# Decay and cosine products written back into PSUM; sine product and low parts of weights on GpSimd; new orders

## The chip, the core and the metric

The kernel runs on one core of one Trainium2 chip. The metric is the time of one execution on the device in microseconds (us), lower is better. The kernel before took 289.08 us, the median of three runs (288.9, 289.08, 290.38).

## What is computed

A pre-norm transformer block in float32 on x of shape (4, 256, 256), four sequences of 256 tokens, with linear ("lightning") attention. There are 16 query heads, 4 key and value heads of 128, rotary positions and a decay for each head.

```python
h = layernorm(x)
q, k, v = h @ wq.T, h @ wk.T, h @ wv.T           # 16, 4 and 4 heads of 128
q, k = rope(q), rope(k)                          # z * cos + rot(z) * sin; rot swaps the halves of 128
# chunked scan in the reference; the same as, for each head with lam = 2**(-8*i/16):
o[i] = sum over j <= i of exp(-lam * (i - j)) * (q[i] . k[j]) * v[j]
x = x + concat(o) @ wo.T
h = layernorm(x)
hidden = fwht(silu(h @ W1.T) * (h @ W3.T))       # Walsh-Hadamard transform over 1024
x = x + hidden @ W2.T
```

## The kernel before

Matrix products keep float32 accuracy by splitting each operand into a high part (a copy rounded to the matmul format fp32r) and a low part (the operand minus its high part). Each product is then three matmuls: high by high, high by low, low by high (`product`, L264 to L266). So every tensor that goes into TensorE (PE) costs a copy on ScalarE (ACT) for the high part and a subtraction on VectorE (DVE) or GpSimd (POOL) for the low part.

The tokens are worked in two halves of 512 (two sequences each). A **unit** u = 0..15 is one pair of heads of one half: u = 8c + p. There are eight PSUM banks. Projections (the items X, K, Q, V in the list `LIN`) land in banks 0 and 1 by turns after the start, in all eight at the start; the scores of a unit stand in banks 2 to 4, the attention output in bank 5, the output projection in 6 and 7. The pipeline of a unit is:

- PE projects the two query heads of unit u + 2 (`queries(u)`), and in even units the key head too (`key(u)`, heads are shared by two units). The item for p = 5 also turns the next normalized half (`turned`). An item may be projected only when the item two places earlier has left its bank (`lin_free`).
- Rotary: ACT copies the two halves of the bank crosswise into `rope_b` (`swap`, L494 and L495). DVE multiplies the bank by the cosine into `rope_a` (L752) and `rope_b` by the sine in place (L753) (`rotate`). POOL adds the two into `qk` (`rope_add`, L629). ACT takes the high part (L500), POOL the low part (`low_rope`, L636).
- Scores: PE writes three banks. DVE multiplies each by the decay table into `p_raw` (`mask`, L775). ACT takes the high part `p_hi` (L507). The low part `p_lo` comes from DVE for the first two (L780), from POOL for the third, S_FIRST1 (L641).
- PE multiplies by the values (`attend`), ACT and DVE split the output (`o_hi` L511, `o_lo` L785), and PE projects it (`project_out`).
- Weights come in 16 chunks of 128x1024. ACT takes the high part (L474) and DVE the low part (L727), one chunk at the end of each of units 0 to 5 and of 9, 11, 12 and 13. PE may use a chunk when `w_lo_done` has reached it: the queries projected in unit 2 need chunk 5, those of unit 4 need chunk 7.

The order on each engine is written out by hand: each engine's block walks over the same loop of units, with helpers called in a fixed order, and every engine executes strictly in that order. An instruction whose semaphore is not there holds all behind it on its engine. After the units comes the feed-forward part, in which PE is fed without rotary work.

## Time and profile before

| | |
|---|---|
| timed runs | 288.9, 289.08, 290.38 us; median 289.08 |
| span of the profiled execution | 287.6 us |
| PE busy | 261.9 us, 91% (1480 matmuls) |
| DVE busy | 229.2 us, 80% |
| POOL busy | 175.0 us, 61% |
| ACT busy | 164.5 us, 57% |
| granted TensorE clock | full in all 40 slices |

The page gives no time for the profiled execution other than its span, which lies 1.5 us under the median of the timed runs. The share of busy time is a mean over very different stages: up to about 11 us everything waits for the first loads and the norm, from there to about 210 us run the 16 units, in which four engines work together, and after that PE is busy nearly without a break while the others idle. DVE shows 9 in every tenth digit from 7% to 40% of the span, PE mostly 7 to 9 there. A busy digit says nothing on who waits for whom; for that the waits and the starts of single instructions are read.

### The profile page before, as it was taken

How to read it: one execution, taken by the hardware profiler on the slowest of the kernel's cores; microseconds unless marked ns; L12 is line 12 of the kernel's file. 1: busy time of each engine (PE TensorE's matmuls, PEld its weight loads, DVE VectorE, ACT ScalarE, POOL GpSimd, SP SyncE). 2: the span in 40 equal slices, each digit the busy share in tenths (PEclk: the TensorE clock that was granted, in tenths of full speed). 3: DMA queues.
4: the chain of work that ended last, by engine and by line, in shares of the span. 5: the costliest groups of instructions: out<-in, count | busy, mean ns of one | idle time of the engine just before them, and what ended most of it. 6: DMA issues, size and time to landing. Idle time of an engine off the chain costs nothing.

```text
span 287.6 us, 4155 instructions
## 1 busy us (share of the span) xinstructions
PE 261.9 (91%) x1480; PEld 226.0 (79%) x1480; DVE 229.2 (80%) x324; ACT 164.5 (57%) x271; POOL 175.0 (61%) x117
## 2 busy tenths in 40 slices
PE   0897898997997999889999979969999999999995
PEld 0685677885896888778898878859888889988885
DVE  2878999999999999876989999999667686234323
ACT  2586776669475686556668658486445453033320
POOL 1049799789975978955687897969795610000000
PEclk9999999999999999999999999999999999999999
DMA  7694020211102020000001002200000000110002
GB/s 269 228 370 135 2 74 1 73 32 43 73 2 74 5 70 1 0 2 0 1 13 63 0 2 73 74 0 2 0 2 0 0 3 0 39 36 0 2 0 73
DMA packets 5203, 13.23 MB, mean 46 GB/s; under 512 B 576, under 2 KB 2112, under 8 KB 5184
## 3 DMA queue, kind: packets, MB, share of 16 engines
q1 hardware_dynamic: 4752, 12.65, 12.4%
q10 hardware_dynamic: 432, 0.33, 0.3%
q8 instruction: 12, 0.20, 0.3%
q14 instruction: 7, 0.06, 0.1%
HBM read 11.93 MB, written 1.05 MB: 45 GB/s over the span
## 4 chain that ended last, share of the span: by engine, by line
PE 34%; DVE 34%; POOL 13%; issue 12%; ACT 4%; DMA 1%; DVEq 0%; SPq 0%; POOLq 0%; ACTq 0%
PE bank L264 11%; PE bank L265 11%; PE bank L266 11%; DVE p_lo L780 7%; DVE rope_b L753 6%; POOL qk L629 6%; DVE p_raw L775 5%; DVE rope_a L752 5%; POOL q_hid L636 4%; DVE xn L721 3%; DVE w_lo L727 3%; DVE o_lo L785 2%; POOL k_lo L636 2%; ACT p_hi L507 1%; DMA x_sb<-in_x 1%
## 5 line engine op out<-in xcount | busy, mean ns | idle before, releaser
L629 POOL TENSOR_TENSOR qk<-rope_a,rope_b 128x512 f32<-128x512 f32 x40 | 66.9, 1687 | 18.9 <-DVE rope_b L753 18.8
L264 PE MATMUL bank<-xt_hi,w_hi 128*128 128x512 f32 x144 | 58.5, 407 | 5.2 <-DVE rope_a L752 3.8
L265 PE MATMUL bank<-xt_lo,w_hi 128*128 128x512 f32 x144 | 57.2, 397 | 0.0
L266 PE MATMUL bank<-xt_hi,w_lo 128*128 128x512 f32 x144 | 57.1, 397 | 0.0
L636 POOL TENSOR_TENSOR q_hid<-qk,q_hid 128x512 fp32r<-128x512 f32 x32 | 48.6, 1529 | 4.0 <-ACT q_hid L500 3.9
L780 DVE TENSOR_TENSOR p_lo<-p_raw,p_hi 128x512 fp32r<-128x512 f32 x32 | 40.1, 1255 | 3.0 <-ACT p_hi L507 2.6
L507 ACT ACTIVATE p_hi<-p_raw 128x512 fp32r<-128x512 f32 x48 | 30.1, 626 | 15.4 <-DVE p_raw L775 14.8
L264 PEld LDWEIGHTS bank<-xt_hi,w_hi 128*128 128x128 f32 x144 | 27.6, 192 | 13.5 <-DVE rope_a L752 5.5
L641 POOL TENSOR_TENSOR p_lo<-p_raw,p_hi 128x512 fp32r<-128x512 f32 x16 | 25.9, 1617 | 20.2 <-ACT p_hi L507 20.1
L753 DVE TENSOR_TENSOR rope_b<-rope_b,sin_sb 128x512 f32<-128x512 f32 x40 | 36.8, 919 | 0.0
L265 PE MATMUL bank<-w_lo,o_hi 128*128 128x256 f32 x128 | 36.2, 283 | 0.0
L266 PE MATMUL bank<-w_hi,o_lo 128*128 128x256 f32 x128 | 36.2, 283 | 0.0
L264 PE MATMUL bank<-w_hi,o_hi 128*128 128x256 f32 x128 | 36.1, 282 | 0.0
L494 ACT ACTIVATE rope_b<-bank 64x512 f32<-64x512 f32 x40 | 23.8, 596 | 17.6 <-POOL qk L629 12.5
L500 ACT ACTIVATE q_hid<-qk 128x512 fp32r<-128x512 f32 x32 | 20.1, 628 | 23.0 <-POOL qk L629 22.3
L266 PEld LDWEIGHTS bank<-xt_hi,w_lo 128*128 128x128 f32 x144 | 27.6, 192 | 6.1
L752 DVE TENSOR_TENSOR rope_a<-bank,cos_sb 128x512 f32<-128x512 f32 x40 | 27.1, 678 | 6.0 <-ACT rope_b L495 5.9
L775 DVE TENSOR_TENSOR p_raw<-bank,decay_sb 128x512 f32<-128x512 f32 x48 | 31.4, 677 | 0.5 <-PE bank L266 0.4
L265 PEld LDWEIGHTS bank<-xt_lo,w_hi 128*128 128x128 f32 x144 | 27.7, 192 | 5.0
L264 PE MATMUL bank<-q_hid,k_hi 128*128 128x512 f32 (+1 forms) x64 | 22.5, 352 | 5.2 <-POOL k_lo L636 5.1
L799 DVE TENSOR_TENSOR rope_b<-bank,rope_a 128x512 f32<-128x512 f32 x16 | 11.0, 689 | 19.6 <-ACT rope_a L518 19.6
L518 ACT ACTIVATE rope_a<-bank 128x512 f32<-128x512 f32 x16 | 9.6, 600 | 27.6 <-PE bank L266 27.6
(70 smaller groups left out, 611.6 us busy)
## 6 DMA issues: line engine op xcount, KB each, us to landing
w_raw<-in_w SPq DMA_DIRECT2D x6, 512.0 KB, 3.2
w_raw<-in_wq SPq DMA_DIRECT2D x4, 512.0 KB, 4.8
decay_sb<-in_decay SPq DMA_DIRECT2D x4, 512.0 KB, 5.9
w_raw<-in_wo SPq DMA_DIRECT2D x4, 512.0 KB, 3.3
x_sb<-in_x SPq DMA_DIRECT2D x4, 256.0 KB, 4.6
out<-x_sb SPq DMA_DIRECT2D x8, 128.0 KB, 1.8
w_raw<-in_wk SPq DMA_DIRECT2D x1, 512.0 KB, 4.8
w_raw<-in_wv SPq DMA_DIRECT2D x1, 512.0 KB, 6.6
```

The source lines that it names most:

```text
L264: pe.matmul(o, a_hi, b_hi, start=first, stop=False, skip_group_check=shared)
L265: pe.matmul(o, a_hi, b_lo, start=False, stop=False, skip_group_check=shared)
L266: return pe.matmul(o, a_lo, b_hi, start=False, stop=last, skip_group_check=shared)
L494: act.activation(rope_b[0:h, r % 2, :], lin_bank(n)[h:P], ACT.Copy)
L507: act.activation(p_hi[:, s, :], p_raw[:, n % 2, :], ACT.Copy).then_inc(p_hi_done, 1)
L629: pool.tensor_tensor(qk[:, r % 2, :], rope_a[:, r % 2, :], rope_b[:, r % 2, :], ALU.add).then_inc(rope_sum, 1)
L636: pool.tensor_tensor(lo, qk[:, r % 2, :], hi.bitcast(F32), ALU.subtract).then_inc(rope_lo, 1)
L641: pool.tensor_tensor(p_lo[:, s, :], p_raw[:, n % 2, :], p_hi[:, s, :].bitcast(F32), ALU.subtract).then_inc(p_lo_pool, 1)
L752: dve.tensor_tensor(a, src, c, ALU.mult).then_inc(lin_free, 1)
L753: dve.tensor_tensor(b, b, s, ALU.mult).then_inc(rope_parts, 1)
L775: dve.tensor_tensor(dst, src, table, ALU.mult).then_inc(mask_done, 1)
L780: dve.tensor_tensor(p_lo[:, s, :], p_raw[:, n % 2, :], p_hi[:, s, :].bitcast(F32), ALU.subtract).then_inc(p_lo_dve, 1)
```

## The change

Four things change.

1. The decay product of the first two score banks and the cosine product are written back into the PSUM bank that they come from. `p_hi`, `p_lo` (first two) and the rotary add then read PSUM. `rope_a` is gone (the feed-forward part's buffer is now called `gate`), and a score bank is free only after its low part (`p_lo_dve`), a projection bank only after the rotary add.
2. The rotary add moves from POOL to DVE (`rotated`), the sine product from DVE to POOL (`times_sine`).
3. The low parts of the weight chunks from chunk 3 on move from DVE to POOL (`low_weights` on POOL), at the end of POOL's unit.
4. All four engines get new orders.

```diff
-        rope_a = sb("rope_a", [P, 2, TOK])
+        gate = sb("gate", [P, 2, TOK])
         rope_b = sb("rope_b", [P, 2, TOK])
...
@@ -311,8 +291,10 @@
                 ks, qs = p // PPG % 2, p % 2
                 needed = max(ROPE_NO[("Q", c, 2 * p + 1)], ROPE_NO[("K", c, p // PPG)])
                 pe.wait_ge(rope_lo, needed + 1)
-                if u:
-                    pe.wait_ge(mask_done, 3 * (u - 1) + s + 1)
+                if u and s == S_FIRST1:
+                    pe.wait_ge(mask_done, 3 * u)
+                elif u:
+                    pe.wait_ge(p_lo_dve, 2 * (u - 1) + s + 1)
...
-                if b == 0:
-                    pe.wait_ge(p_lo_dve, 2 * (u + 1))
-                else:
+                pe.wait_ge(p_lo_dve, 2 * (u + 1))
+                if b:
                     pe.wait_ge(p_lo_pool, u + 1)
...
@@ -489,14 +470,14 @@
                 n, r = LIN_NO[item], ROPE_NO[item]
                 act.wait_ge(lin_full, n + 1)
                 if r >= 2:
-                    act.wait_ge(rope_sum, r - 1)
+                    act.wait_ge(lin_free, LIN_NO[ROPE[r - 2]] + 1)
...
             def high_rope(item):
                 r = ROPE_NO[item]
-                act.wait_ge(rope_sum, r + 1)
+                act.wait_ge(lin_free, LIN_NO[item] + 1)
                 act.activation(rope_dst(item)[0], qk[:, r % 2, :], ACT.Copy).then_inc(rope_hi, 1)
 
             def high_p(u, s):
@@ -504,7 +485,8 @@
                 act.wait_ge(mask_done, n + 1)
                 if u and s == S_SECOND:
                     act.wait_ge(o_full, 2 * u)
-                act.activation(p_hi[:, s, :], p_raw[:, n % 2, :], ACT.Copy).then_inc(p_hi_done, 1)
+                src = p_raw[:, u % 2, :] if s == S_FIRST1 else s_bank[s][:]
+                act.activation(p_hi[:, s, :], src, ACT.Copy).then_inc(p_hi_done, 1)
...
-            high_weights(3)
             swap(("K", 0, 0))
             swap(("Q", 0, 0))
+            high_rope(("K", 0, 0))
             high_v(0, 0)
-            high_rope(("K", 0, 0))
             swap(("Q", 0, 1))
+            high_rope(("Q", 0, 0))
             high_v(0, 1)
-            high_rope(("Q", 0, 0))
+            high_weights(3)
             swap(("Q", 0, 2))
+            high_rope(("Q", 0, 1))
             high_v(0, 2)
-            high_rope(("Q", 0, 1))
             swap(("Q", 0, 3))
+            high_rope(("Q", 0, 2))
             high_v(0, 3)
-            high_rope(("Q", 0, 2))
-            high_p(0, S_FIRST0)
             high_rope(("Q", 0, 3))
-            high_p(0, S_SECOND)
             for u in range(UNITS):
-                if u:
-                    before = queries(u - 1)
-                    fill(key(u - 1) + turned(u - 1))
-                    for item in before[:1]:
-                        high_rope(item)
-                    high_p(u, S_FIRST0)
-                    for item in before[1:]:
-                        high_rope(item)
-                    high_o(u - 1, 1)
-                    high_p(u, S_SECOND)
-                fill(values(u)[:2] + queries(u)[:1])
+                fill(key(u - 1) + turned(u - 1) if u else [])
+                high_p(u, S_FIRST0)
+                high_p(u, S_SECOND)
                 for item in key(u - 1) if u else []:
                     high_rope(item)
-                fill(queries(u)[1:])
+                if u:
+                    high_o(u - 1, 1)
+                fill(values(u)[:1])
                 high_p(u, S_FIRST1)
+                fill(values(u)[1:2] + queries(u))
                 if u in (UNITS - 2, UNITS - 1):
                     silu(u - UNITS + 2)
                 fill(values(u)[2:3])
+                for item in queries(u)[:1]:
+                    high_rope(item)
                 high_o(u, 0)
+                for item in queries(u)[1:]:
+                    high_rope(item)
                 fill(values(u)[3:])
                 if unit_chunk(u) is not None:
                     high_weights(unit_chunk(u))
...
-            def rope_add(item):
+            def times_sine(item):
                 r = ROPE_NO[item]
-                pool.wait_ge(rope_parts, r + 1)
-                if r >= 2:
-                    pool.wait_ge(rope_lo, r - 1)
-                pool.tensor_tensor(qk[:, r % 2, :], rope_a[:, r % 2, :], rope_b[:, r % 2, :],
-                                   ALU.add).then_inc(rope_sum, 1)
+                pool.wait_ge(swapped, r + 1)
+                b = rope_b[:, r % 2, :].rearrange("p (b t) -> p b t", b=BH)
+                pool.tensor_tensor(b, b, sin_sb[:].unsqueeze(1).broadcast_to([P, BH, SEQ]),
+                                   ALU.mult).then_inc(sin_done, 1)
...
-            def low_p(u, s):
-                n = 3 * u + s
-                pool.wait_ge(p_hi_done, n + 1)
-                pool.tensor_tensor(p_lo[:, s, :], p_raw[:, n % 2, :], p_hi[:, s, :].bitcast(F32),
+            def low_weights(n):
+                _, _, at = CHUNKS[n]
+                pool.wait_ge(w_lo_done, n)
+                pool.wait_ge(w_hi_done, n + 1)
+                pool.tensor_tensor(w_lo[:, at:at + CH], w_raw[:, n % SLOTS, :], w_hi[:, at:at + CH].bitcast(F32),
+                                   ALU.subtract).then_inc(w_lo_done, 1)
+
+            def low_p(u):
+                pool.wait_ge(p_hi_done, 3 * (u + 1))
+                pool.tensor_tensor(p_lo[:, S_FIRST1, :], p_raw[:, u % 2, :], p_hi[:, S_FIRST1, :].bitcast(F32),
                                    ALU.subtract).then_inc(p_lo_pool, 1)
...
-            rope_add(("K", 0, 0))
-            rope_add(("Q", 0, 0))
+            pool.wait_ge(tables_loaded, 48)
+            times_sine(("K", 0, 0))
+            times_sine(("Q", 0, 0))
             low_rope(("K", 0, 0))
-            rope_add(("Q", 0, 1))
+            times_sine(("Q", 0, 1))
             low_rope(("Q", 0, 0))
+            times_sine(("Q", 0, 2))
             low_rope(("Q", 0, 1))
-            rope_add(("Q", 0, 2))
-            rope_add(("Q", 0, 3))
+            times_sine(("Q", 0, 3))
             low_rope(("Q", 0, 2))
+            low_weights(3)
             low_rope(("Q", 0, 3))
             for u in range(UNITS):
-                if u:
-                    before = queries(u - 1)
-                    for item in before[:1]:
-                        low_rope(item)
-                    if u % PAIRS == 3:
-                        inverse_deviation(u // PAIRS + 1)
-                    for item in key(u - 1):
-                        rope_add(item)
-                    for item in before[1:] + key(u - 1):
-                        low_rope(item)
-                low_p(u, S_FIRST1)
+                before = key(u - 1) if u else []
+                for item in before:
+                    times_sine(item)
+                if u % PAIRS == 3:
+                    inverse_deviation(u // PAIRS + 1)
+                for item in before:
+                    low_rope(item)
+                low_p(u)
                 for item in queries(u):
-                    rope_add(item)
+                    times_sine(item)
+                for item in queries(u):
+                    low_rope(item)
+                if unit_chunk(u) is not None:
+                    low_weights(unit_chunk(u))
...
-            def rotate(item):
+            def times_cosine(item):
 
                 n, r = LIN_NO[item], ROPE_NO[item]
                 dve.wait_ge(swapped, r + 1)
+                o = lin_bank(n)[:].rearrange("p (b t) -> p b t", b=BH)
+                dve.tensor_tensor(o, o, cos_sb[:].unsqueeze(1).broadcast_to([P, BH, SEQ]),
+                                  ALU.mult).then_inc(cos_done, 1)
+
+            def rotated(item):
+
+                n, r = LIN_NO[item], ROPE_NO[item]
+                dve.wait_ge(cos_done, r + 1)
+                dve.wait_ge(sin_done, r + 1)
                 if r >= 2:
-                    dve.wait_ge(rope_sum, r - 1)
-                src, a, b = (m.rearrange("p (b t) -> p b t", b=BH)
-                             for m in (lin_bank(n)[:], rope_a[:, r % 2, :], rope_b[:, r % 2, :]))
-                c, s = (tb[:].unsqueeze(1).broadcast_to([P, BH, SEQ]) for tb in (cos_sb, sin_sb))
-                dve.tensor_tensor(a, src, c, ALU.mult).then_inc(lin_free, 1)
-                dve.tensor_tensor(b, b, s, ALU.mult).then_inc(rope_parts, 1)
+                    dve.wait_ge(rope_lo, r - 1)
+                dve.tensor_tensor(qk[:, r % 2, :], lin_bank(n)[:], rope_b[:, r % 2, :],
+                                  ALU.add).then_inc(lin_free, 1)
...
-                if s == S_FIRST1:
-                    dve.wait_ge(p_lo_dve, 2 * u + 1)
-                elif u and s == S_FIRST0:
-                    dve.wait_ge(p_lo_dve, 2 * u)
-                elif u:
-                    dve.wait_ge(p_lo_pool, u)
+                if s == S_FIRST1 and u >= 2:
+                    dve.wait_ge(p_lo_pool, u - 1)
...
-                    dst = p_raw[:, n % 2, :].rearrange("p (b h t) -> p b h t", b=BH, h=2)
                 else:
                     src = s_bank[s][:].rearrange("p (h t) -> p h t", h=2)
-                    dst = p_raw[:, n % 2, :].rearrange("p (h t) -> p h t", h=2)
+                dst = p_raw[:, u % 2, :].rearrange("p (h t) -> p h t", h=2) if s == S_FIRST1 else src
                 dve.tensor_tensor(dst, src, table, ALU.mult).then_inc(mask_done, 1)
...
             def low_p(u, s):
                 n = 3 * u + s
                 dve.wait_ge(p_hi_done, n + 1)
-                dve.tensor_tensor(p_lo[:, s, :], p_raw[:, n % 2, :], p_hi[:, s, :].bitcast(F32),
+                dve.tensor_tensor(p_lo[:, s, :], s_bank[s][:], p_hi[:, s, :].bitcast(F32),
                                   ALU.subtract).then_inc(p_lo_dve, 1)
...
+            times_cosine(("K", 0, 0))
+            times_cosine(("Q", 0, 0))
             fill(START[2:5])
-            low_weights(3)
-            fill(START[5:])
-            mask(0, S_FIRST0)
-            mask(0, S_SECOND)
-            low_p(0, S_FIRST0)
-            low_p(0, S_SECOND)
+            for h in range(1, 4):
+                times_cosine(("Q", 0, h))
+                fill([("Q", 0, h), ("V", 0, h)])
             for u in range(UNITS):
+                before = key(u - 1) if u else []
+                mask(u, S_FIRST0)
+                mask(u, S_SECOND)
+                for item in before:
+                    times_cosine(item)
+                low_p(u, S_FIRST0)
+                fill(before + turned(u - 1) if u else [])
+                low_p(u, S_SECOND)
                 if u:
-                    mask(u, S_FIRST0)
-                    mask(u, S_SECOND)
-                    fill(key(u - 1) + turned(u - 1))
-                    low_p(u, S_FIRST0)
                     low_o(u - 1, 1)
-                    low_p(u, S_SECOND)
                 fill(values(u)[:1])
                 mask(u, S_FIRST1)
                 if u == PAIRS + 1:
                     add_attention(0, 1)
-                fill(values(u)[1:2] + queries(u))
+                fill(values(u)[1:2])
+                for item in queries(u):
+                    times_cosine(item)
+                fill(queries(u))
...
-                if unit_chunk(u) is not None:
-                    low_weights(unit_chunk(u))
```

POOL around unit 0 and 1, before. `qk<-rope_a,rope_b` is the rotary add, `q_hid` and `k_lo` take low parts.

```order
L641 TENSOR_TENSOR p_lo<-p_raw,p_hi 128x512
L629 TENSOR_TENSOR qk<-rope_a,rope_b 128x512 x2
L636 TENSOR_TENSOR q_hid<-qk,q_hid 128x512
L629 TENSOR_TENSOR qk<-rope_a,rope_b 128x512
L636 TENSOR_TENSOR q_hid<-qk,q_hid 128x512
L636 TENSOR_TENSOR k_lo<-qk,k_hi 128x512
L641 TENSOR_TENSOR p_lo<-p_raw,p_hi 128x512
```

POOL at the same place in the changed kernel. `rope_b<-rope_b,sin_sb` is the sine product.

```order
L620 TENSOR_TENSOR w_lo<-w_raw,w_hi 128x1024
L614 TENSOR_TENSOR q_hid<-qk,q_hid 128x512
L625 TENSOR_TENSOR p_lo<-p_raw,p_hi 128x512
L607 TENSOR_TENSOR rope_b<-rope_b,sin_sb 128x512 x2
L614 TENSOR_TENSOR q_hid<-qk,q_hid 128x512 x2
L620 TENSOR_TENSOR w_lo<-w_raw,w_hi 128x1024
L607 TENSOR_TENSOR rope_b<-rope_b,sin_sb 128x512
L614 TENSOR_TENSOR k_lo<-qk,k_hi 128x512
L625 TENSOR_TENSOR p_lo<-p_raw,p_hi 128x512
```

Between two low parts `p_lo` there now stands a chunk of weights, ahead of the key's sine product; both query low parts stand ahead of the chunk.

DVE in unit 1 (from the two decay products on), before.

```order
L775 TENSOR_TENSOR p_raw<-bank,decay_sb 128x512 x2
L752 TENSOR_TENSOR rope_a<-bank,cos_sb 128x512
L753 TENSOR_TENSOR rope_b<-rope_b,sin_sb 128x512
L780 TENSOR_TENSOR p_lo<-p_raw,p_hi 128x512
L785 TENSOR_TENSOR o_lo<-bank,o_hi 128x512
L780 TENSOR_TENSOR p_lo<-p_raw,p_hi 128x512
L775 TENSOR_TENSOR p_raw<-bank,decay_sb 128x512
L752 TENSOR_TENSOR rope_a<-bank,cos_sb 128x512
L753 TENSOR_TENSOR rope_b<-rope_b,sin_sb 128x512
```

DVE in unit 1 of the changed kernel, from the key's cosine product on.

```order
L735 TENSOR_TENSOR bank<-bank,cos_sb 128x512
L769 TENSOR_TENSOR p_lo<-bank,p_hi 128x512
L745 TENSOR_TENSOR qk<-bank,rope_b 128x512
L769 TENSOR_TENSOR p_lo<-bank,p_hi 128x512
L774 TENSOR_TENSOR o_lo<-bank,o_hi 128x512
L764 TENSOR_TENSOR p_raw<-bank,decay_sb 128x512
L735 TENSOR_TENSOR bank<-bank,cos_sb 128x512 x2
L745 TENSOR_TENSOR qk<-bank,rope_b 128x512 x2
L774 TENSOR_TENSOR o_lo<-bank,o_hi 128x512
```

The key's add (`qk<-bank,rope_b`), which needs POOL's sine product, now stands ahead of the second `p_lo`, of `o_lo` and of the third decay product. The same holds for the queries' two adds and the `o_lo` behind them.

ACT at the start of the changed kernel, from the swap of the second query on: the high part of weight chunk 3 now stands behind the second values' high part; before it stood ahead of all swaps.

```order
L475 ACTIVATE rope_b<-bank 64x512
L476 ACTIVATE rope_b<-bank 64x512
L481 ACTIVATE q_hid<-qk 128x512
L465 ACTIVATE v_hid<-bank 128x512
L455 ACTIVATE w_hi<-w_raw 128x1024
L475 ACTIVATE rope_b<-bank 64x512
L476 ACTIVATE rope_b<-bank 64x512
```

Every following swap at the start stands behind that chunk.

## Rows read from the trace of the kernel before

**Rows 1.** Busy time by engine in three stretches; columns as the first line says.

```profile
core 0: us, PE busy (x) PEld busy (x) DVE busy (x) ACT busy (x) POOL busy (x), PEclk, DMA share, GB/s
10.76:96.66 85.90, 77.50 (x399) 64.11 (x399) 82.03 (x106) 61.23 (x100) 67.75 (x43) 1.00 0.24 87
96.66:194.70 98.04, 92.66 (x538) 80.53 (x537) 90.30 (x122) 65.16 (x111) 77.79 (x50) 1.00 0.07 22
194.70:287.60 92.90, 89.57 (x540) 79.80 (x538) 51.74 (x83) 34.55 (x58) 28.11 (x20) 1.00 0.04 12
```

**Rows 2.** What PE waited for, 10.76 to 96.66: us, times, longest.

```profile
PE bank L264 <- POOL k_lo L636: 2.7, 2, 1.6
PE bank L264 <- DVE rope_a L752: 2.1, 3, 1.7
```

**Rows 3.** Groups of the page: shapes, count, busy us, mean ns, idle before, releaser.

```profile
L629 POOL TENSOR_TENSOR qk<-rope_a,rope_b 128x512 f32<-128x512 f32 x40 | 66.9, 1687 | 18.9 <-DVE rope_b L753 18.8
L636 POOL TENSOR_TENSOR q_hid<-qk,q_hid 128x512 fp32r<-128x512 f32 x32 | 48.6, 1529 | 4.0 <-ACT q_hid L500 3.9
L780 DVE TENSOR_TENSOR p_lo<-p_raw,p_hi 128x512 fp32r<-128x512 f32 x32 | 40.1, 1255 | 3.0 <-ACT p_hi L507 2.6
L641 POOL TENSOR_TENSOR p_lo<-p_raw,p_hi 128x512 fp32r<-128x512 f32 x16 | 25.9, 1617 | 20.2 <-ACT p_hi L507 20.1
L753 DVE TENSOR_TENSOR rope_b<-rope_b,sin_sb 128x512 f32<-128x512 f32 x40 | 36.8, 919 | 0.0
L494 ACT ACTIVATE rope_b<-bank 64x512 f32<-64x512 f32 x40 | 23.8, 596 | 17.6 <-POOL qk L629 12.5
L500 ACT ACTIVATE q_hid<-qk 128x512 fp32r<-128x512 f32 x32 | 20.1, 628 | 23.0 <-POOL qk L629 22.3
```

**Rows 4.** The same by line and shape: weights, and the low part that reads PSUM.

```profile
L727 DVE TENSOR_TENSOR w_lo<-w_raw,w_hi 128x1024 fp32r<-128x1024 f32 x14 | 22.2, 1588 | 0.5 <-ACT w_hi L474 0.5
L785 DVE TENSOR_TENSOR o_lo<-bank,o_hi 128x512 fp32r<-128x512 f32 x32 | 21.8, 680 | 2.3 <-ACT o_hi L511 2.1
L474 ACT ACTIVATE w_hi<-w_raw 128x1024 fp32r<-128x1024 f32 x14 | 14.6, 1051 | 4.1 <-DMA w_raw<-in_wk 3.1 <-DMA w_raw<-in_wq 1.0
```

**Rows 5.** POOL, single instructions: start, us, instruction, idle before and releaser.

```profile
42.93 1.68 POOL L629 TENSOR_TENSOR qk<-rope_a,rope_b 128x512 f32<-128x512 f32 x1 [0.63 <-DVE rope_b L753]
...
65.11 1.02 POOL L622 TENSOR_TENSOR rstd<-var_eps,minus_half 128x4 f32<-128x4 f32 x1
...
204.70 1.29 POOL L641 TENSOR_TENSOR p_lo<-p_raw,p_hi 128x512 fp32r<-128x512 f32 x1 [1.90 <-ACT p_hi L507]
205.95 1.30 POOL L659 TENSOR_TENSOR xn<-w_raw 128x512 f32<-128x512 f32 x1
```

**Rows 6.** POOL's low part of the third scores: of units 0, 2 and 5.

```profile
35.49 1.62 POOL L641 TENSOR_TENSOR p_lo<-p_raw,p_hi 128x512 fp32r<-128x512 f32 x1 [1.90 <-ACT p_hi L507]
...
58.66 1.30 POOL L641 TENSOR_TENSOR p_lo<-p_raw,p_hi 128x512 fp32r<-128x512 f32 x1 [2.51 <-ACT p_hi L507]
...
96.57 1.75 POOL L641 TENSOR_TENSOR p_lo<-p_raw,p_hi 128x512 fp32r<-128x512 f32 x1
```

**Rows 7.** ACT at the start: its swap of the first query.

```profile
16.25 0.60 ACT L494 ACTIVATE rope_b<-bank 64x512 f32<-64x512 f32 x1 [0.34 <-PE bank L266]
```

**Rows 8.** PE, single matmuls: start, us, instruction, idle before and releaser.

```profile
25.96 0.50 PE L264 MATMUL bank<-w_hi,xt_hi 128*128 128x512 f32 x1 [1.46 <-DVE v_hid L739]
...
52.36 0.39 PE L264 MATMUL bank<-xt_hi,w_hi 128*128 128x512 f32 x1
...
57.95 0.50 PE L264 MATMUL bank<-xt_hi,w_hi 128*128 128x512 f32 x1
...
94.92 0.34 PE L277 MATMUL bank<-ident_sb,xn 128*128 128x128 f32 x1
...
96.66 0.50 PE L264 MATMUL bank<-q_hid,k_hi 128*128 128x512 f32 x1
```

**Rows 9.** DVE's low part of weight chunk 5.

```profile
50.32 1.71 DVE L727 TENSOR_TENSOR w_lo<-w_raw,w_hi 128x1024 fp32r<-128x1024 f32 x1
```

25 lines of the change are left out of this document (12 added, 13 removed).

## The prediction, made before the changed kernel ran

> **What bounds the kernel now.** I read the busy time by stretch first. It cuts the run in three after a start of 10.8 us: the first six units (10.76 to 96.66), units 6 to 13 (to 194.70) and the rest [rows 1]. PE is idle for 85.90 - 77.50 = 8.4 us in the first, 98.04 - 92.66 = 5.4 in the second and 92.90 - 89.57 = 3.3 in the last. So PE is already the main bound, and all that a relief of the other engines can win is about 8.4 + 5.4 = 13.8 us, plus some tenths behind. Next, the waits of PE: in the first stretch it waits for POOL's low part of the key and for DVE's cosine product, by which a projection bank comes free, 4.8 us together [rows 2]. DVE, at 82.03 of 85.90 us, has no slack there, POOL some (67.75). The groups show why DVE is full: its operations with both inputs in SBUF are stretched (1255 ns for p_lo, 919 for the sine product), while the same size read from PSUM takes 680 [rows 3, 4]. POOL is stretched as well: an add takes 1.68 us beside DVE's work and such an operation follows the one before by 1.25 (205.95 - 204.70) when alone [rows 5].
>
> **Part by part: busy time.** DVE loses 40 sine products of 919 ns (36.8 us) and 11 of 14 weight chunks of 1588 ns (17.5 us). It gains 40 adds of about 0.65 (26 us), since they read a bank, and its 32 p_lo fall from 1255 to about 650 ns (19 us). Sum: about 47 us less [rows 3, 4]. A sine product takes the add's place on POOL one for one (40 each). POOL gets 11 chunks. No row shows a 128x1024 on POOL: the lower bound is 1.25 us (one 128x512), the upper 3.4 (two at 1.69); I take two uncontended ones, 2.5, since nothing in DVE's new steady work reads two SBUF inputs. So POOL: 96 operations at 1.25 in place of 141 us (66.9 + 48.6 + 25.9, the 8 key low parts besides), plus 27.5. Its total hardly changes; only its content does. PE's and ACT's work is the same. Busy time alone would therefore say faster. The page "SBUF — State Buffer" of the Trainium skill (section "Who interferes with whom") says that a DVE instruction with two SBUF inputs contends with a GpSimd one that reads SBUF and one with at most one SBUF input does not. The trace agrees (1.68 against 1.25). Were it otherwise, the POOL steps below would grow by 0.35 each. The skill's "GPSIMD Engine Reference" gives 4497 ns for 2048 elements of a float32 add (section "Reconciling with measured numbers"), an estimate of 2.25 us for a chunk; no trace here shows it, and the sum would be 1 us smaller by it.
>
> **Part by part: the chain.** What counts is which engine holds which in its order. Steps: POOL 1.25, DVE on a bank 0.65, ACT copy 0.63, ACT swap 2 x 0.6 = 1.2, ACT high part of a chunk 1.05 [rows 3 to 5], and 0.05 from a step on one engine to the next on another. I follow POOL's low part p_lo of the third scores from unit to unit; before, it starts at 35.49, 58.66 and 96.57 in units 0, 2 and 5: 61.1 us from 0 to 5 [rows 6].
>
> Interval without a key ahead (into units 2 and 4), from the moment its high part is there: two swaps 2.4 (now behind that high part), the second cosine product 0.65 (ahead of the first add), add 0.65 = 3.7; high parts of query and output 1.25, o_lo 0.65 = 5.6; two decay products 1.3; ACT's second p_hi 0.63, p_lo 0.65, o_lo 0.65, third decay product 0.65, its high part 0.63 = 10.1; with ten hand-overs 10.5 us.
>
> Interval with a key (into units 1, 3 and 5), on POOL: p_lo, two sine products 3.75; a bubble of 0.6, since the first query's high part comes only 3.7 + 0.63 in; two low parts 2.5; the weight chunk 2.5; the key's sine product 1.25 = 10.6. Only then DVE adds the key (0.65), and behind that add stand p_lo, o_lo and the third decay product: key's high part 0.63, o_hi 0.63, o_lo 0.65, product 0.65, high part 0.63 = 14.4, with few hand-overs 14.6 us. This is the step that I hold decisive: the chunk sits ahead of the key's sine product, and the add that waits for it sits ahead of the next unit's scores on DVE.
>
> Sum from unit 0 to 5: 3 x 14.6 + 2 x 10.5 + the rstd of unit 3, 1.0 [rows 5], and some statistics 0.5 = 66.3, against 61.1: 5.2 us later. POOL waits in it, so its spare time does not help.
>
> The start: swap of the first query at 16.25 [rows 7], done 17.45; cosine product and the key's add 1.3, key's high part and first values 1.23, swap 1.2, high parts of query and values 1.2, chunk 3 on ACT 1.05 (it stood ahead of all swaps), swap 1.2, sine product 1.25, add and low part of the third values 1.3 = 27.2 to 27.5 with hand-overs. PE's last values wait for that; they ran at 25.96 [rows 8]: 1.4 late. From there values 1.4, their high and low part 1.3, two decay products 1.3, p_hi 0.63, p_lo 0.65, product 0.65, high part 0.63: the first POOL p_lo at about 34.4, 1.1 us before its 35.49, since DVE's contended p_lo pair is gone. So unit 5's p_lo starts at 34.4 + 66.3 = 100.7.
>
> PE at the end of unit 5: the first turn of the normalized half needs the bank of unit 5's first query, free only after its add, 3.9 behind: 104.6. Before, this turn ran at 94.92 and the scores of unit 6 followed at 96.66 [rows 8]: 1.74 later, so now 106.3, 9.7 us late. Steps queued on one engine run a little closer than I set them (0.60 for 0.65), so I take 8.5. Bounds: -8.4 (all of PE's idle time gone) and 8.5 + 9 (POOL stretched as before: in each of three key intervals six operations 0.35 more and the chunk 0.9 more). Within this, the queries of unit 2 wait for chunk 5: DVE had it at 50.32 + 1.71 = 52.03 and they ran at 52.36 without a wait [rows 8, 9]; on POOL it ends about 8.5 to 9.5 behind unit 1's p_lo (34.4 + 14.6 = 49.0), 58. The same for chunk 7 in unit 4.
>
> Units 6 to 13: the old waits (5.4) go. New ones come, because a bank now waits for sine product and add: in an even unit the key's projection follows the first query's by 57.95 - 52.36 = 5.6 us [rows 8], and the bank comes free about 1.6 (projection and decay of the third scores behind it) + 1.1 + 3.7 = 6.4: 0.8 to 1.2 in units 6, 10 and 12, some 2 for the third values of unit 8, which follow the queries by only 4.2, and up to 3.3 at the turn in unit 13, behind two chunks. At most 9, against 5.4. I take no change, with -5.4 and +3.7 as the ends. The rest: no rotary work, PE at 96%; the butterflies on POOL start behind p_lo of unit 14 as now. 0, within 1.
>
> **Sum.** 8.5 + 0 + 0 on a span of 287.6: 296.1. The median of the timed runs lies 1.5 above the span of before: 297.6, rounded to 297.
>
> **Rivals.** *PE runs near its own work (faster).* DVE has 47 us less to do and POOL's operations are short; if hand-overs are cheaper than mine and PE leads the others by enough, the chunk on POOL is hidden in the lead. It decides if two successive intervals of POOL's p_lo take under 23.2 us (58.66 - 35.49) and PE does not wait for chunks 5 and 7. It wins 4 to 14 of the 13.8 us: 275 to 286, centre 280. For it: the busy times. Against: the order, in which every wait for a sine product blocks DVE. *A wash.* The first units lose 5, the later ones win their 5.4: 288 to 291. *POOL stays stretched.* If an operation of DVE on PSUM still holds POOL up, or a chunk takes 3.4: 305 to 308. Against it: the add at 1.25 alone. That DVE and ACT work in PSUM is slower than in SBUF is no case of its own: 680 ns is in the sum.
>
> **Numbers.** What tells a change from none here is 0.5%, 1.4 us. Forecast 292 to 304: 60%. POOL stretched, over 304: 8%. Wash: 10%, of which 6 within 0.5% and 4 slower. PE near its own work: 22%, about 10 of it below 280. Slower 60 + 8 + 4 = 72%, same 6%, faster 22%. The range leaves out 10% below 280 and 8% above 304; the forecast's own range is 292 to 304.
>
> **What would show it.** Right: POOL at about 1.25 to 1.3 us for each 128x512; 24 to 26 us for two successive intervals of p_lo in the first six units; PE waiting for `w_lo` at the queries of units 2 and 4, for `qk` at the turn of unit 5 and at the keys; DVE idle ahead of adds, waiting for POOL; unit 6's scores on PE at 103 to 107. Wrong: those scores before 96.7, no wait of PE for `w_lo`, or DVE still above 95% busy there. If POOL's chunk is near 1.3 us, or PE does its second stretch in under 94 us, my sum fails in that term.

## The result: 309.4 us, slower, and later than the forecast

The changed kernel takes 309.4 us, the median of four runs (306.8 to 313.78); the kernel before took 289.24 beside it. The ratio is 1.065, 95% interval 1.061 to 1.069. The forecast was 297.0 us with a range of 280 to 304: slower, as forecast, but 12.4 us beyond it and 5.4 beyond the range.

The spans of its executions differ more than those of the kernel before, from 303.8 to 312.0 us, and the granted clock with them (0.989 to 0.951). The rows below come from the execution of 303.8 us, the fastest of eight, unless the text says "the slower execution": that is the one of 312.0, with the clock most disturbed, which counts in the median but not in the ratio and is used only to show what the clock costs.

The three stretches, cut at the first scores of units 6 and 14 as in [rows 1]. Columns: stretch, its length, busy us of each engine with instruction counts, granted clock, DMA share, GB/s.

```profile
10.76:106.00 95.24, 79.12 (x398) 65.24 (x399) 64.16 (x101) 60.84 (x101) 71.65 (x52) 0.96 0.22 78
106.00:211.56 105.56, 93.15 (x539) 80.65 (x538) 74.19 (x118) 64.48 (x111) 71.40 (x54) 1.00 0.06 21
211.56:303.80 92.24, 89.28 (x541) 79.77 (x539) 47.35 (x81) 34.25 (x57) 23.63 (x18) 1.00 0.04 12
```

Against before: +9.34 us, +7.52, -0.66; together the 16.2 us between the spans. DVE's busy time fell by 17.9 us in the first stretch (in all from 229.2 to 191.1, 38 us, where about 47 were computed: the groups that changed lose 46 us, but neighbouring instructions overlap in the record, 16 us in all before and 9 after), and it bought nothing: PE now idles 16.1 us there instead of 8.4, and 12.4 instead of 5.4 in the second.

The groups of the changed kernel that answer to [rows 3, 4]:

```profile
L607 POOL TENSOR_TENSOR rope_b<-rope_b,sin_sb 128x512 f32<-128x512 f32 x40 | 51.1, 1290 | 13.0 <-ACT rope_b L476 12.9
L620 POOL TENSOR_TENSOR w_lo<-w_raw,w_hi 128x1024 fp32r<-128x1024 f32 x11 | 26.5, 2409 | 0.0
L745 DVE TENSOR_TENSOR qk<-bank,rope_b 128x512 f32<-128x512 f32 x40 | 27.4, 686 | 6.5 <-issue 3.7 <-POOL rope_b L607 1.6 <-DVE bank L735 0.6
L769 DVE TENSOR_TENSOR p_lo<-bank,p_hi 128x512 fp32r<-128x512 f32 x32 | 21.6, 686 | 5.6 <-ACT p_hi L489 5.1
```

POOL's operations are no longer stretched (1290 ns where the add took 1687), and a chunk takes 2.41 us there, between my bounds of 1.25 and 3.4 and near the 2.5 taken. DVE's p_lo and add take 686 ns each. So every duration in the sum held.

What DVE waited for at the two new operations (us, times, longest):

```profile
DVE bank L735 <- ACT rope_b L476: 37.4, 32, 2.3
DVE qk L745 <- issue: 3.7, 11, 1.3
DVE qk L745 <- POOL rope_b L607: 1.6, 3, 0.7
```

The time that DVE gained is spent ahead of the cosine product, waiting for ACT's swap (5.9 us, 6 times, before). ACT now makes the swaps of the queries behind the third p_hi. At the adds DVE hardly waits for POOL.

What PE waited for in units 6 to 13 (us, times, longest), first before (96.66 to 194.70, where 1.2 us more in two waits follow these), then in the changed kernel (106.00 to 211.56):

```profile
PE bank L264 <- POOL k_lo L636: 2.4, 2, 1.5
PE bank L264 <- DVE rope_a L752: 1.7, 1, 1.7
```

```profile
PE bank L244 <- DVE qk L745: 6.4, 5, 1.6
PE bank L257 <- DVE qk L745: 2.9, 2, 2.7
PE bank L244 <- DVE o_lo L774: 2.6, 3, 1.0
PE bank L244 <- DVE v_hid L726: 0.5, 1, 0.5
```

`qk` on L745 is the rotary add, behind which a projection bank comes free. The waits for `k_lo` and `rope_a` are gone and 12.4 us of others stand in their place.

Single matmuls of PE, answering to [rows 8]: last values of the start, queries of unit 2, turn of the next half in unit 5, scores of unit 6.

```profile
26.54 0.50 PE L244 MATMUL bank<-w_hi,xt_hi 128*128 128x512 f32 x1 [2.85 <-DVE v_hid L726]
...
57.40 0.47 PE L244 MATMUL bank<-xt_hi,w_hi 128*128 128x512 f32 x1 [1.70 <-issue]
...
104.76 0.66 PE L257 MATMUL bank<-ident_sb,xn 128*128 128x128 f32 x4 [2.77 <-DVE qk L745]
...
106.00 0.47 PE L244 MATMUL bank<-q_hid,k_hi 128*128 128x512 f32 x1
```

POOL around unit 1, answering to [rows 5, 6]; the last chunk shown, at 54.92, is chunk 5 (before, on DVE, it stood in [rows 9]).

```profile
33.45 1.30 POOL L625 TENSOR_TENSOR p_lo<-p_raw,p_hi 128x512 fp32r<-128x512 f32 x1 [1.04 <-ACT p_hi L489]
...
40.36 2.41 POOL L620 TENSOR_TENSOR w_lo<-w_raw,w_hi 128x1024 fp32r<-128x1024 f32 x1
42.70 1.32 POOL L607 TENSOR_TENSOR rope_b<-rope_b,sin_sb 128x512 f32<-128x512 f32 x1
...
48.02 1.29 POOL L625 TENSOR_TENSOR p_lo<-p_raw,p_hi 128x512 fp32r<-128x512 f32 x1 [1.17 <-ACT p_hi L489]
...
54.92 2.38 POOL L620 TENSOR_TENSOR w_lo<-w_raw,w_hi 128x1024 fp32r<-128x1024 f32 x1
...
58.73 1.30 POOL L625 TENSOR_TENSOR p_lo<-p_raw,p_hi 128x512 fp32r<-128x512 f32 x1 [1.43 <-ACT p_hi L489]
```

Chunk 5 ends at 54.92 + 2.38 = 57.30 and the queries of unit 2 start at 57.40: the wait that the page puts down to "issue" is the wait for the weights. The starts of POOL's p_lo lie 14.6 and then 10.7 us apart.

### The profile page after: what moved, and what is told of

Its sections match the earlier page's. It is cut to its first block, busy times and chain, and to the rows that moved or that the text cites. A ratio compares the mean times of both kernels' runs of the same rounds, so it can differ in the third digit from the quotient of the medians.

```text
span 312.0 us, 4122 instructions
## 1 busy us (share of the span) xinstructions
PE 273.4 (88%) x1480; PEld 235.2 (75%) x1480; DVE 190.9 (61%) x313; ACT 163.7 (52%) x271; POOL 168.0 (54%) x128
## 4 chain that ended last, share of the span: by engine, by line
PE 46%; POOL 19%; DVE 15%; ACT 12%; issue 6%; DMA 1%; SPq 0%; DVEq 0%; ACTq 0%; POOLq 0%
PE bank L244 15%; PE bank L246 14%; PE bank L245 14%; POOL rope_b L607 11%; POOL p_lo L625 5%; ACT p_hi L489 3%; DVE xn L708 3%; DVE p_raw L764 3%; ACT o_hi L493 2%; ACT q_hid L481 2%; DVE bank L764 2%; PE bank L257 2%; DVE qk L745 2%; DVE o_lo L774 2%; DVE p_lo L769 2%
## 5 line engine op out<-in xcount | busy, mean ns | idle before, releaser
L244 PE MATMUL bank<-xt_hi,w_hi 128*128 128x512 f32 x144 | 59.8, 415 | 11.9 <-DVE qk L745 8.9
L607 POOL TENSOR_TENSOR rope_b<-rope_b,sin_sb 128x512 f32<-128x512 f32 x40 | 51.1, 1290 | 15.6 <-ACT rope_b L476 15.5
L735 DVE TENSOR_TENSOR bank<-bank,cos_sb 128x512 f32<-128x512 f32 x40 | 27.9, 697 | 40.1 <-ACT rope_b L476 40.1
L614 POOL TENSOR_TENSOR q_hid<-qk,q_hid 128x512 fp32r<-128x512 f32 x32 | 40.9, 1299 | 11.6 <-ACT q_hid L481 11.6
L489 ACT ACTIVATE p_hi<-bank 128x512 fp32r<-128x512 f32 x32 | 19.2, 599 | 28.7 <-PE bank L246 14.6
L745 DVE TENSOR_TENSOR qk<-bank,rope_b 128x512 f32<-128x512 f32 x40 | 27.4, 685 | 6.1 <-issue 3.1
L774 DVE TENSOR_TENSOR o_lo<-bank,o_hi 128x512 fp32r<-128x512 f32 x32 | 22.0, 689 | 10.1 <-ACT o_hi L493 10.1
L244 PE MATMUL bank<-p_hi,v_hid 128*128 128x512 f32 x64 | 22.1, 345 | 6.4 <-DVE o_lo L774 6.4
L620 POOL TENSOR_TENSOR w_lo<-w_raw,w_hi 128x1024 fp32r<-128x1024 f32 x11 | 26.5, 2405 | 0.0
L764 DVE TENSOR_TENSOR bank<-bank,decay_sb 128x512 f32<-128x512 f32 x32 | 21.2, 691 | 7.2 <-PE bank L246 7.2
L769 DVE TENSOR_TENSOR p_lo<-bank,p_hi 128x512 fp32r<-128x512 f32 x32 | 21.6, 684 | 6.2 <-ACT p_hi L489 5.7
```

The costliest lines, as they stand in the source:

```text
L244: pe.matmul(o, a_hi, b_hi, start=first, stop=False, skip_group_check=shared)
L489: act.activation(p_hi[:, s, :], src, ACT.Copy).then_inc(p_hi_done, 1)
L607: pool.tensor_tensor(b, b, sin_sb[:].unsqueeze(1).broadcast_to([P, BH, SEQ]), ALU.mult).then_inc(sin_done, 1)
L614: pool.tensor_tensor(lo, qk[:, r % 2, :], hi.bitcast(F32), ALU.subtract).then_inc(rope_lo, 1)
L735: dve.tensor_tensor(o, o, cos_sb[:].unsqueeze(1).broadcast_to([P, BH, SEQ]), ALU.mult).then_inc(cos_done, 1)
L745: dve.tensor_tensor(qk[:, r % 2, :], lin_bank(n)[:], rope_b[:, r % 2, :], ALU.add).then_inc(lin_free, 1)
```

## The experiments

Four explanations stood at the start, and the expectations number them: (1) the weight chunk ahead of the key's sine product (my decisive step); (2) the new rotary step, by which DVE's row waits for POOL, with `o_lo` and the next scores behind it; (3) the bank that is now held until the add; (4) the new orders themselves, on ACT above all. Later two more questions came up, the clock and the wait at the key's bank.

Seven of the results below are slower than every range that was written down for them: chunks back on DVE, output's split ahead, only the rotary step, the old rotary step in the new orders, decay product and chunks in the old orders, and the two runs ahead of the table of parts. One is faster (the chunk behind the key's sine product) and one lies between its two ranges (the key behind the scores).

Times are medians; each ratio is to the kernel before on the same chip, with its 95% interval. "u6" and "u14" are the starts of the scores of units 6 and 14 on PE in the profiled execution (before: 96.66 and 194.70; changed: 106.00 and 211.56).

### The changed kernel again

The same kernel, without an edit.

> The changed kernel once more, beside the variants: 306 to 311 us; its profile is to show how much of the extra time is PE busy (clock below full) and how much is PE idle.

Measured: 309.48 us, 1.073 (1.068 to 1.078). The rows shown above are from its execution of 303.8 us.

### Chunks back on DVE

The low parts of the weight chunks return to DVE, at the place they had before.

```diff
-                if unit_chunk(u) is not None:      # POOL
-                    low_weights(unit_chunk(u))
...
+                if unit_chunk(u) is not None:      # DVE, behind values(u)[3:]
+                    low_weights(unit_chunk(u))
```

> The changed kernel with the low parts of all weight chunks back on VectorE, at their old places; the rest as changed. Rival 1, the step that the prediction held decisive (the chunk on POOL ahead of the key's sine product): the intervals of POOL's p_lo with a key fall from 14.6 to about 12, the waits for chunks 5 and 7 (1.3 and 1.0 us) and the clock falls behind them go: 296 to 300 us. Theory 2, a chain that runs through the rotary adds on DVE, o_lo, attend on PE and the second p_hi, whatever stands on POOL: the key intervals of units 6 to 13, most of which have no chunk ahead, are 13.1 already, so only the chunk waits and about 1 us in each of units 3 and 5 go: 303 to 307 us.

Measured: 322.35 us, 1.115 (1.113 to 1.118), u6 113.6, u14 227.4. Thirteen us worse: the interval of p_lo without a key grows from 10.7 to 13.2, and the one behind unit 7, which has no chunk, stays at 11.1. A chunk on DVE stands in the same circle of waits. With the new orders the chunks are better off on POOL. It does not tell whether the chunk's place ahead of the key's sine product costs anything; a later experiment does.

### Output's split ahead of the queries

```diff
+                high_o(u, 0)
-                for item in queries(u)[:1]:
+                for item in queries(u):
                     high_rope(item)
-                high_o(u, 0)
-                for item in queries(u)[1:]:
-                    high_rope(item)
```

and on DVE `low_o(u, 0)` ahead of both adds (but in unit 8).

> The changed kernel with o_hi and o_lo of the first sequence ahead of the queries' high parts (ACT) and rotary adds (DVE) in each unit but 8. Theory 2 (o_lo behind the adds delays attend, and by it the second p_hi of the next unit): intervals of p_lo fall by about 1 us, PE's wait for o_lo (6.4 us) goes: 298 to 304 us. Rival 3 (the projection bank, held until the add, is what PE loses by): the adds come 0.6 later, PE's waits for qk (10.1 us by the profile) grow by 0.6 for each key: 309 to 314 us.

Measured: 319.43 us, 1.105 (1.100 to 1.110). What PE waited for:

```profile
PE bank L244 <- DVE qk L743: 15.7, 8, 3.0
PE bank L244 <- issue: 9.3, 3, 4.2
PE bank L257 <- DVE qk L743: 5.9, 2, 3.4
```

The waits for o_lo (6.3 us) are gone, and those for a bank (`qk`, 15.5 to 21.6 us) and for the weights (3.0 to 9.3) grew by more: what is taken ahead on DVE pushes the adds back, and a bank is held until its add.

### Only the decay product in PSUM

The kernel before, with the decay product of the first two banks written back into PSUM, and nothing else of the change.

```diff
-                dve.tensor_tensor(p_lo[:, s, :], p_raw[:, n % 2, :], ...
+                dve.tensor_tensor(p_lo[:, s, :], s_bank[s][:], ...
...
-                act.activation(p_hi[:, s, :], p_raw[:, n % 2, :], ACT.Copy)
+                src = p_raw[:, u % 2, :] if s == S_FIRST1 else s_bank[s][:]
+                act.activation(p_hi[:, s, :], src, ACT.Copy)
```

> The kernel before with one part alone: the decay product of the first two score banks in place in PSUM, p_hi and p_lo read from there, in the old order. If the loss is in the rotary part and this part only relieves DVE (p_lo from 1.25 to 0.68 us, POOL's operations less stretched): 282 to 287 us. If holding the score banks until p_lo costs PE as much: 288 to 292 us.

Measured: 284.47 us, 0.983 (0.979 to 0.986): **faster than both kernels**. Its stretches:

```profile
10.76:96.12 85.36, 77.00 (x399) 65.10 (x399) 74.26 (x106) 60.80 (x101) 65.08 (x43) 0.98 0.25 88
96.12:190.35 94.23, 91.88 (x540) 80.17 (x538) 81.27 (x122) 64.62 (x112) 71.96 (x50) 1.00 0.07 23
190.35:282.90 92.55, 89.50 (x541) 79.80 (x539) 49.10 (x83) 34.05 (x58) 25.73 (x20) 1.00 0.04 12
```

Nearly all of the gain is in units 6 to 13 (98.04 to 94.23 us), where PE is now busy 91.88 of 94.23 us. It holds the scores' bank longer, and no wait of PE for p_lo shows.

### Only the rotary step

The kernel before with the sine product on POOL, cosine product in the bank and add on DVE (`times_cosine`, `rotated`, `times_sine` as in the diff of the change), each called where `rotate` and `rope_add` stood; for a pair of queries both cosine products come ahead of both adds.

```diff
-            rope_add(("K", 0, 0))
+            times_sine(("K", 0, 0))
...
-                            rotate(item)
+                            times_cosine(item)
+                            rotated(item)
```

> The kernel before with one part alone: cosine product in PSUM, sine product on POOL, add on DVE, in the old order (both queries' cosine products ahead of both adds). Theory 2 and rival 3 (the adds on DVE wait for POOL, and banks come free late): 298 to 312 us, with PE waiting for qk. Rival 1 (the chunk on POOL is the cause; there is none on POOL here): 286 to 291 us.

Measured: 339.16 us, 1.172 (1.165 to 1.180), u6 117.4, u14 242.2. What PE and DVE waited for:

```profile
PE bank L264 <- DVE qk L758: 24.2, 9, 4.3
PE bank L264 <- DVE o_lo L791: 11.1, 5, 2.5
```

```profile
DVE qk L758 <- POOL rope_b L628: 46.0, 33, 2.8
```

33 of 40 adds hold DVE's queue while POOL multiplies. In the old orders this is the most expensive part of the change: before, POOL waited for DVE's products; now DVE's add, with all that stands behind it in DVE's row, waits for POOL.

### Cosine product in SBUF

The changed kernel, but the cosine product goes to SBUF and the bank is free at once, so the add has both inputs in SBUF.

```diff
-                dve.tensor_tensor(o, o, cos_sb..., ALU.mult).then_inc(cos_done, 1)
+                dve.tensor_tensor(a, o, cos_sb..., ALU.mult).then_inc(lin_free, 1)
...
-                dve.tensor_tensor(qk[:, r % 2, :], lin_bank(n)[:], rope_b[:, r % 2, :], ...
+                dve.tensor_tensor(qk[:, r % 2, :], gate[:, r % 2, :], rope_b[:, r % 2, :], ...
```

> The changed kernel with the cosine product written into SBUF, so that the projection bank is free at the cosine product and not at the add; sine product still on POOL, add still on DVE (now from two SBUF tensors), orders as changed. Theory 3 (PE loses by the bank held until the add): PE's waits for the add (10.1 + 5.7 us by the profile) and the clock falls behind them go: 292 to 298 us, less what stretched adds take. Theory 2 (DVE blocked behind the add is the loop, whatever the bank): intervals of p_lo stay 10.7 and 13 to 15, 304 to 310 us. Against both: an add from two SBUF inputs of 1.2 us would lengthen the loop, over 310.

Measured: 319.75 us, 1.103 (1.096 to 1.110), u6 113.6, u14 224.2. The add's group, and PE's largest wait:

```profile
L747 DVE TENSOR_TENSOR qk<-gate,rope_b 128x512 f32<-128x512 f32 x40 | 38.5, 990 | 4.6 <-POOL rope_b L607 2.5 <-issue 1.7 <-DVE gate L737 0.4
```

```profile
PE bank L244 <- DVE o_lo L776: 17.8, 8, 3.4
```

The bank is free at the cosine product and the kernel is no faster: the waits for a bank fall from 15.5 us (`qk`) to 8.0 (`gate`), those for o_lo rise from 6.3 to 17.8. But the edit did a second thing. The add takes 990 ns in place of 686, 11 us more over the 40, and it stands ahead of o_lo in DVE's row. So the run shows that freeing the bank in this way does not pay; what the held bank alone costs it can't tell.

### The old rotary step in the new orders

```diff
-                    times_sine(item)
+                    rope_add(item)
...
-                for item in queries(u):
-                    times_cosine(item)
-                fill(queries(u))
+                fill(queries(u))      # with rotate(item), as before
```

> The changed kernel with the rotary part as before (cosine and sine product on DVE, cosine into SBUF, add on POOL); decay in PSUM, chunks on POOL and the new orders kept. If the rotary move is the whole loss: 280 to 287 us. If the new orders or the chunks on POOL cost something of their own: 288 to 300 us.

Measured: 318.55 us, 1.103 (1.099 to 1.107), u6 115.0, u14 224.4. DVE takes the first p_lo behind the key's rotation here, as before. PE waits 15.7 us for o_lo (10 times) and 8.8 for the weights, DVE 42.8 us for ACT's swaps (26 times). The new orders do not fit the old rotary step.

### The first query's swap ahead of the third p_hi

```diff
+                fill(values(u)[1:2] + queries(u)[:1])
                 high_p(u, S_FIRST1)
-                fill(values(u)[1:2] + queries(u))
+                fill(queries(u)[1:])
```

> The changed kernel with ACT's swap of the first query ahead of the third p_hi. Theory 3: the first query's sine product cannot start before POOL's p_lo, which now waits 1.2 us longer for its high part, so nothing is won for the first bank and the rest comes later: 308 to 314 us. If the swap behind p_hi was the late step: 300 to 306 us.

The split of the second values moves along with the swap. Measured: 313.81 us, 1.086 (1.083 to 1.088): no gain, 4 us worse. DVE's waits:

```profile
DVE bank L736 <- ACT rope_b L476: 30.0, 26, 2.7
DVE qk L746 <- POOL rope_b L608: 19.6, 31, 0.8
```

The waits for the swap fell by 7.4 us and those for POOL's sine product, which stands behind POOL's own p_lo, rose from 1.6 to 19.6. ACT's place of this one swap is not it; the wait passes on to POOL.

### Decay product and chunks in the old orders

> The kernel before with two parts: decay product in PSUM and the chunks on POOL (from chunk 3 on, behind the two rotary adds of the unit), rotary part and orders as before. Against 284.5 us with the decay part alone: DVE has 17 us less to do, POOL 27 more. If DVE is still what holds PE: 278 to 283 us. If POOL, whose low part of the key PE waits for, takes its place: 285 to 292 us.

The edit is the decay one above and the move of the chunks to POOL's end of a unit, `low_weights(unit_chunk(u))` behind the adds. Measured: 293.37 us, 1.015 (1.014 to 1.017). Its first stretch:

```profile
10.76:105.05 94.29, 81.04 (x399) 67.94 (x399) 70.46 (x101) 61.10 (x101) 72.98 (x49) 0.93 0.22 79
```

The chunks on POOL cost 8.9 us here, all of it in units 0 to 5 (94.29 against 85.36). PE idles 4.9 us more, and is busy 4.0 us more for the same 399 matmuls at a granted clock of 0.93 against 0.98. The next longest wait beside k_lo is one of 4.2 us marked "issue", for the weights.

### Output between the two adds

As "output's split ahead", but `low_o(u, 0)` stands between the two adds.

```diff
-                fill(queries(u))
+                fill(queries(u)[:1])
...
                 low_o(u, 0)
+                fill(queries(u)[1:])
```

> The changed kernel with o_hi of the first sequence ahead of both queries' high parts on ACT, and o_lo between the two queries' adds on DVE, so that the first bank is not held longer. If ACT's and DVE's order behind the adds is what delays attend: PE's wait for o_lo goes, its wait for qk stays: 300 to 306 us. If the loss of the variant with the output first came from something else than the bank: 310 to 320 us.

Measured: 313.04 us, 1.083 (1.079 to 1.087). Waits for o_lo 1.2 us instead of 6.3, for `qk` 18.5 instead of 15.5, for the weights 6.9 instead of 3.0. Same pattern, smaller.

### New orders and decay product alone; and all parts in the old orders

The first is the changed kernel with chunks and rotary step both as before, the second the kernel before with the three moves of work and none of the new orders. Both are the edits above put together.

> The new orders with the decay product in PSUM, but rotary part and weight chunks as before. Against the same parts in the old order (284.5 us) it gives the price of the new orders alone. Theory 4 (the new order puts the queries' high parts, which wait for the rotary sum, ahead of o_hi in the same unit): 310 to 325 us. If the loss of the variant with the old rotary part (318.6) came from the chunks on POOL: 285 to 295 us.

> All three moves of the change (decay in PSUM, chunks on POOL, rotary move) in the old orders; against the changed kernel it gives what the new orders do with the same parts. Theory 4 alone would have it faster than 308; with the rotary move in the old order at 339 and DVE relieved of p_lo and chunks, I expect the new orders to win here: 318 to 335 us.

Measured: 332.65 us, 1.152 (1.148 to 1.156), and 336.06 us, 1.161 (1.156 to 1.166). With these the parts can be set beside each other (all with the decay product in PSUM but the one marked):

| | old rotary step | new rotary step |
|---|---|---|
| old orders, chunks on DVE | 284.5 | 339.2 (decay as before) |
| old orders, chunks on POOL | 293.4 | 336.1 |
| new orders, chunks on DVE | 332.7 | 322.4 |
| new orders, chunks on POOL | 318.6 | 309.4 |

The rotary step costs 43 us in the old orders and gains 9 in the new ones (chunks on POOL). The new orders cost 25 us with the old step and gain 27 with the new one. Alone they cost 43 and 25 us, together 16 (293.4 to 309.4): they fit each other, but not well enough to pay for themselves. With the chunks on DVE the new orders cost 48 us with the old step (284.5 to 332.7).

### Old rotary step, new orders, output first on ACT

```diff
+                high_o(u, 0)
-                for item in queries(u)[:1]:
+                for item in queries(u):
                     high_rope(item)
-                high_o(u, 0)
-                for item in queries(u)[1:]:
-                    high_rope(item)
```

> The changed kernel with the rotary step as before (318.6 us), and in addition ACT takes o_hi of the first pair ahead of the high parts of both queries. Theory 4 (in the new order ACT's o_hi stands behind a high part that waits for the rotary sum, and with the old rotary step that sum comes late, from POOL): PE's waits for o_lo fall from 15.7 us (10) to under 7, and the time to 305 to 312. Rival (DVE's part of the order costs it: two rotations, four operations of about 0.7 to 0.9 us, stand ahead of o_lo): the waits for o_lo stay above 12 us and the time within 2 us of 318.6. Rival (the pass-on as in the two orders tried on the changed kernel itself): the waits move to others and the time is over 318.

Measured: 319.12 us, 1.102 (1.095 to 1.110). The waits for o_lo fell from 15.7 to 11.9 us only, those for the weights rose to 9.7, the time is the same. My fourth theory falls: ACT's place of o_hi alone does not explain what the new orders cost with the old step.

### Decay product, and the key first

The fast version above, and ACT takes the key's high part ahead of the first query's swap; the norm is applied to two tiles first instead of one.

```diff
-                fill(values(u)[:2] + queries(u)[:1])
+                fill(values(u)[:2])
                 for item in key(u - 1) if u else []:
                     high_rope(item)
-                fill(queries(u)[1:])
+                fill(queries(u))
```

> The kernel before with only the decay product in PSUM (284.5 us, ratio 0.983), and in addition ACT takes the key's high part ahead of the first query's swap, and the norm's first part covers two of four tiles. Theory: PE's longest waits there are for k_lo on POOL (4.8 us, 3 times 2.0), and the key's high part is what POOL waits for; they fall below 3 us and the time is 281 to 284 (ratio 0.972 to 0.983). Rival (k_lo stands behind POOL's other work, not behind ACT; or the swap that is now later delays the next query): no gain, 284 to 288.

Measured: 287.52 us, 0.994 (0.991 to 0.996): slower than the version it was built on. The waits for k_lo stayed (4.5 us against 4.8), so ACT was not what they hung on, and 2.1 us of waits for p_lo came up that were not there.

### Two pauses in PE's row

The kernel before, with two added waits in the up-projections, where PE works alone.

```diff
-                if n >= 2:
+                if n == 6:
+                    pe.wait_ge(hid_done, n)
+                elif n == 10:
+                    pe.wait_ge(hid_lo_done, n)
+                elif n >= 2:
                     pe.wait_ge(hid_done, n - 1)
```

> The kernel before, with two pauses put into PE's feed-forward part, where it works alone and without a break: ahead of the seventh pair of up-projections it waits also for the product of the sixth (about 1.4 us, computed from silu 0.60, product 0.69 and hand-overs), and ahead of the eleventh for the low part of the tenth (about 3.2 us: high part 0.63 and low part 1.2 more). Theory (the clock falls to its lower level after a pause of 2 us or more and not after one of 1.5, as the rows of the changed kernel read): granted clock 1.00 behind the first pause, 0.5 to 0.7 for 3 to 5 us behind the second, and the time grows by 4.6 for the pauses and 1.5 to 2.5 for the clock, to 295 to 297 (ratio 1.021 to 1.028). Rival (the clock fell in the changed kernel for the mean load there and not for one pause): 1.00 throughout, 293 to 294.5 (ratio 1.014 to 1.019).

Measured: 295.23 us, 1.020 (1.014 to 1.027); span 292.6. The two pauses, and the stretches right behind them (columns as in the first fence):

```profile
234.04 0.47 PE L264 MATMUL bank<-xt_hi,w_hi 128*128 128x512 f32 x1 [2.28 <-DVE rope_b L803]
...
261.41 0.47 PE L264 MATMUL bank<-xt_hi,w_hi 128*128 128x512 f32 x1 [2.90 <-DVE q_hid L808]
```

```profile
234.00:238.00 4.00, 3.96 (x17) 3.30 (x18) 2.29 (x6) 1.50 (x3) 0.00 (x0) 1.00 0.02 6
262.00:266.00 4.00, 4.00 (x19) 3.33 (x18) 0.69 (x1) 0.83 (x2) 0.00 (x0) 1.00 0.00 0
```

The clock stays at 1.00 behind both, and the span grows by 5.0 us, the length of the pauses (5.2). The four executions do not all agree: two have a mean clock of 1.00 and take 294.3 and 294.4 us, in the rival's range; the others have 0.994 and 0.982 (296.1 and 298.8 us), and of the ten of the kernel before beside them the lowest has 0.992. So the rows speak for the undisturbed executions only. In the slower execution of the changed kernel it fell in the midst of the units: PE at the scores and queries of unit 2, and the stretches around them:

```profile
57.55 0.63 PE L244 MATMUL bank<-q_hid,k_hi 128*128 128x512 f32 x1
...
59.92 0.76 PE L244 MATMUL bank<-xt_hi,w_hi 128*128 128x512 f32 x1 [0.88 <-issue]
60.48 0.63 PE L245 MATMUL bank<-xt_lo,w_hi 128*128 128x512 f32 x1
60.91 0.63 PE L246 MATMUL bank<-xt_hi,w_lo 128*128 128x512 f32 x1
```

```profile
46.00:58.00 12.00, 10.12 (x60) 8.69 (x59) 8.07 (x14) 7.41 (x14) 8.66 (x8) 0.96 0.14 45
58.00:61.00 3.00, 2.12 (x6) 1.24 (x5) 2.48 (x4) 1.54 (x3) 1.82 (x1) 0.50 0.06 14
61.00:65.00 4.00, 4.00 (x15) 3.18 (x14) 0.70 (x1) 1.52 (x4) 2.14 (x2) 0.63 0.33 121
```

0.50 is the lower level, 1.2 GHz, and a matmul of 512 columns follows the one before by 0.43 us there (60.91 - 60.48) instead of 0.23. So a pause of 2.9 us in PE's row did not bring the clock down in this execution. In the slower execution of the changed kernel it was down already at 57.55, ahead of the wait for chunk 5 and behind one pause of 1.88 us (for o_lo, up to 56.24), the whole of PE's idle time in the 12 us up to 58. My reading, that a pause over 2 us is what does it, falls.

### The weight chunk behind the key's sine product

```diff
                 for item in before:
                     times_sine(item)
+                if before and unit_chunk(u - 1) is not None:
+                    low_weights(unit_chunk(u - 1))
...
-                if unit_chunk(u) is not None:
+                if unit_chunk(u) is not None and not key(u):
                     low_weights(unit_chunk(u))
```

> The changed kernel (309.4 us), but in units with a key POOL takes the weight chunk behind the key's sine product instead of ahead of it (units 0, 2, 4 and 12). If my decisive step was right, the add of the key comes 2.4 us earlier; the intervals of POOL's p_lo with a key fall from 14.6 to 15.9 towards the 13.1 of the key units without a chunk, unit 6's scores run at 101 to 103 on PE instead of 106.0, and the time is 304 to 307. Rival (the chunk only fills time that POOL has while PE's attention and the bank set the interval; the key's low part now stands behind the chunk in its place): intervals within 0.5 of before, 308 to 311.

Measured: 301.95 us, 1.045 (1.041 to 1.049), u6 102.5, u14 207.5. That is 7.5 us better than the changed kernel (5.9 by the two ratios, 1.045 and 1.065; in the traces 4.0: span 299.8 against 303.8, of which 3.5 are gained by the scores of unit 6). POOL in unit 1:

```profile
41.65 1.29 POOL L607 TENSOR_TENSOR rope_b<-rope_b,sin_sb 128x512 f32<-128x512 f32 x1 [0.88 <-ACT rope_b L476]
42.91 2.40 POOL L620 TENSOR_TENSOR w_lo<-w_raw,w_hi 128x1024 fp32r<-128x1024 f32 x1
45.45 1.29 POOL L614 TENSOR_TENSOR k_lo<-qk,k_hi 128x512 fp32r<-128x512 f32 x1
```

The intervals with a key and a chunk fall from 14.6, 15.1, 15.9 and 15.8 us to 14.1, 14.0, 14.7 and 13.7. The step held decisive is shown, but a chunk's 2.4 us ahead of the key bought 0.5 to 2.1 us when taken away: behind it stood other work nearly as late.

### The key behind the scores, and both

```diff
                     scores(u, S_SECOND)
+                    if u:
+                        fill(key(u - 1))
...
-                    fill(values(u)[3:] + key(u) + turned(u))
+                    fill(values(u)[3:] + turned(u))
```

> The changed kernel, but PE projects the key of an even unit behind the first two scores of the next unit instead of ahead of them, since its bank comes free 1.2 to 1.7 us too late there. If the waits for banks are what made units 6 to 13 take 105.6 us and not the 98 I put in, the waits for qk at the keys go, the scores run 1.2 to 1.7 us earlier in each of units 7, 9, 11 and 13, that stretch takes 100 to 102 us, and the time is 303 to 306. Rival (another step of the same cycle, the key's sine product and add, then comes 1.5 us later and holds p_lo and o_lo behind it on DVE): no gain, 308 to 312, with more waits for o_lo.

> The changed kernel with both of these moves. If each cause stands on its own the gains add up: 298 to 303 us. If both sit on the one cycle through the key's add, they do not: within 2 us of the better of the two.

Measured: the key alone 307.16 us, 1.062 (1.056 to 1.067), u6 106.2, u14 212.1; both moves 301.11 us, 1.041 (1.039 to 1.043). Units 6 to 13 of the first:

```profile
106.24:212.10 105.86, 95.01 (x539) 82.32 (x537) 74.41 (x118) 65.11 (x112) 71.87 (x54) 0.97 0.06 21
```

105.86 us where it was 105.56. From one unit's first scores to the next, PE is faster into units 7, 9, 11 and 13 (for instance 9.9 us instead of 12.7 into unit 7) and loses it into units 8, 10, 12 and at the turn (11.2 instead of 9.8 into unit 8). Its idle time falls from 12.4 to 10.9 us, and 1.9 us of longer busy time at a clock of 0.97 take that back. So removing the wait at the key's bank gives back 1.6 of the 7 us of added idle time: it is mostly one place of a longer circle, as the rival has it, though the time lies between the two ranges. The two moves together are 0.8 us better than the chunk's alone, which is within the intervals; in the traces units 6 to 13 take 103.4 us with both and 105.0 with the chunk's alone.

## Where the prediction failed: right in its sign, 12 us short

The sum was 8.5 + 0 + 0 on 287.6, and 1.5 behind. Measured: +9.34, +7.52 and -0.66 in the trace, and 309.4 - 303.8 = 5.6 between that span and the median.

**Durations.** Right: POOL at 1.29 for each 128x512, 2.41 for a chunk, DVE at 0.69. The page "SBUF — State Buffer" of the Trainium skill ("Who interferes with whom") says the add with one input in PSUM leaves POOL alone and one with two SBUF inputs does not; the trace agrees (POOL 1687 to 1290 ns). With both inputs of the add in SBUF it was the add that grew, from 686 to 990 ns, while POOL's sine product stayed at 1301. The estimate from the Trainium skill's page "GPSIMD Engine Reference" ("Reconciling with measured numbers"), 2.25 us for a chunk, lies 0.16 under the measured 2.41. The price put on a stretched POOL step, 0.35 us, was a little under what the rows give (1687 against 1290 ns, 0.40); it stood in the upper bound only.

**The chain of the first six units.** Right at its end to within a microsecond, in part by luck. First p_lo 33.45 (computed 34.4); interval with a key 14.6, 15.1, 15.9 (computed 14.6), without one 10.7 and 11.2 (10.5); unit 5's p_lo 101.02 (100.7); the turn 104.76 (104.6); the scores of unit 6 at 106.00 (106.3, and 105.2 with the discount). I had the start 0.9 us too late (values at 26.54, computed 27.4) and the five intervals 1.3 us too short together, which cancelled. The discount of 1.2 us, taken because steps queued on one engine run closer, was not earned. The waits for chunks 5 and 7 came. One sign did not: "DVE idle ahead of adds, waiting for POOL" is 1.6 us in the whole kernel, and "issue" 3.7; DVE idles 37.4 us ahead of the cosine products, for ACT's swaps. The chain had these swaps in it (2.4 us an interval), so the sum held, but the rival's counter-argument, that every wait for a sine product blocks DVE, described the old orders (46.0 us there) and not these.

**The decisive step.** Right as to its place, too dear as to its size: the chain put the whole chunk (2.5 us) into every key interval, and moving it away gave 0.5 to 1.2 us in the first units. That the 14.6 came true is luck: the path without the chunk is 14.0 to 14.7 long, slower than I had it.

**Units 6 to 13: the step that failed.** I wrote "the old waits (5.4) go. New ones come", counted them to "at most 9, against 5.4" and then took no change, with +3.7 as the upper end. The old waits went. The bank waits came to 6.4 + 2.9 = 9.3 us, all of the "at most 9", and nearly place by place: 1.21, 1.56 and 1.20 at the keys of units 6, 10 and 12, 1.17 at the third values of unit 8, 2.9 at the turn, and 1.28 at a query of unit 13 that I had not counted. Beside them stand 2.6 us of waits for o_lo, which I had not put in at all, and 0.5 for the values. The difference in idle time is 12.4 - 5.4 = 7.0, and PE is busy 0.5 us longer. Two errors, then: the middle between two ends was taken although all that spoke for the lower end was that the count might be high; and a wait was counted for each bank alone, while the add that frees the bank stands in DVE's row ahead of the o_lo that PE's attention needs. In even units PE waits for both. None of these edits shortened this stretch of 105.6 us: bank freed early, the waits go to o_lo (110.6 us, with the longer add in it); o_lo first, they go to the banks (107.7 in both versions); first swap earlier, to POOL's sine product (108.3); key later, to the next unit (105.9).

**The clock and the spread: a term that was missing.** Full in all slices before, the clock was no term of the sum. The changed kernel's eight executions lie at 0.951 to 0.989, their spans at 303.8 to 312.0 us, so the median is 5.6 us over the span of the best, where before it was 1.5 (a time is about 1.8 us longer than its span in both kernels). Four of them have 0.989 and take 303.8 to 306.7 us, the four from 0.978 down 308.4 to 312.0. So the clock goes with the longer ones; for the 2.9 us between executions of the same mean clock the record shows no cause. Between the execution of 303.8 and the one of 312.0, PE's busy time for the same 1480 matmuls goes from 264.0 to 273.4 us. It is part of other results too: 4 of the 9 us of the chunks in the old orders. What brings it down is not settled: pauses of 2.3 and 2.9 us did not in the feed-forward part, and neither did 12.4 us of idle time over units 6 to 13 of the execution read here (1.00).

**The account.** 297.6 forecast, + 0.8 in the first stretch, + 7.5 in the second, - 0.7 in the third, + 4.1 between profile and median (5.6 - 1.5; 3.3 without the slower execution) = 309.3, measured 309.4. That it closes is no proof, since it splits the measured time at the same cuts.

**The rivals.** PE near its own work: no; two intervals took 25.3 us, over its 23.2, and PE waited for both chunks. A wash: no. POOL stays stretched: its time, 305 to 308, comes nearest, but its mechanism is refuted by the 1290 ns. The chances were fair on the sign; the range failed at its upper end, because the second stretch came out 3.8 us above its own bound of +3.7 and nothing stood for the clock and the spread (4.1). The second stretch alone would have made it 305, just outside, the spread alone 302, inside.

**What stays open.** Why the new orders cost 25 us with the old rotary step: ACT's place of o_hi is not enough. The swaps behind the third p_hi are a candidate that was not tried there (DVE waits 42.8 us for them, against 19.8 in the old orders with the same parts). What the held bank costs by itself. And what lowers the clock in the units. The parts were tried in sets, not each edit of the orders by itself.

## What to carry to other kernels

Where four engines hand one unit of work around in hand-written rows, busy time taken off one of them gains nothing unless it shortens the circle of waits: a step that makes a full row (DVE's) wait for another engine's product holds everything behind it in that row. The largest such wait need not be the one expected: here it was 46.0 us for POOL's product in the old orders and 37.4 for ACT's swap in the new ones. Try the parts of a change alone; here the smallest of them, a product written back into the bank it came from, gains 1.7% by itself and the others bury it. When new waits have been counted, put the count into the sum, and ask for every instruction that now waits which operand of PE stands behind it.

## What the runs showed of the hardware

TensorE's clock fell in the midst of a working kernel. It was granted in full in all slices of the profile before. In the changed kernel it was 0.96 on average over the first stretch, in which PE idled 16.1 us instead of 8.4, and fell to 0.50, the lower of its two levels, for some microseconds at a time in the slower execution. In the kernel with only the new rotary step, where PE idled 22.2 and 24.1 us in the first two stretches, it was lower still:

```profile
10.76:117.43 106.67, 84.43 (x399) 70.86 (x399) 70.28 (x108) 62.34 (x101) 58.26 (x45) 0.89 0.19 70
117.43:242.15 124.72, 100.61 (x539) 86.62 (x537) 76.53 (x122) 65.72 (x110) 62.03 (x49) 0.92 0.06 18
```

So PE paid twice there: it waited longer, and the 539 matmuls of units 6 to 13 kept it busy for 100.61 us instead of 92.66 (538 in the record before). That the waits bring the clock down is not shown. In the changed kernel 12.4 us of idle time in units 6 to 13 had no such price, nor had the pauses of 2.3 and 2.9 us in the feed-forward part.

An add on DVE with one input in PSUM took 686 ns for 128x512 and 990 with both in SBUF. POOL's operations of that size took 1290 ns in the changed kernel and 1687 (the add) before, beside DVE's operations with two inputs in SBUF.
